# Values of a softmax group in four stretches, a fifth place for exponentials, row DMAs ahead of gathers

## The reference

```python
def _L0_attn_b_ref(x, Wq, Wk, Wv, Wo):
    ...
    q, k, v = (proj(Wq), proj(Wk), proj(Wv))      # 16 heads of 16
    ...                                           # rotary turn of q and k
    att = jnp.einsum('bhqd,bhkd->bhqk', q, k) / math.sqrt(hd)
    mask = jnp.triu(jnp.full((T, T), -jnp.inf, dtype=att.dtype), k=1)
    att = jax.nn.softmax(att + mask, axis=-1)
    out = jnp.einsum('bhqk,bhkd->bhqd', att, v)
    out = out.transpose(0, 2, 1, 3).reshape(B, T, D)
    return out @ Wo.T
x = x + _L0_attn_b_ref(_layernorm(x, axis=-1), L0_attn_b_Wq, L0_attn_b_Wk, L0_attn_b_Wv, L0_attn_b_Wo)
```

## Time and profile before

| | us |
|---|---|
| median of 3 runs (1100.65 to 1104.69) | 1101.19 |
| the profiled execution | 1101.02 |
| its span, first to last instruction | 1099.3 |
| TensorE busy | 1047.7 (95%) |
| ScalarE busy | 617.4 (56%) |
| VectorE busy | 594.2 (54%) |
| GpSimd busy | 489.3 (45%) |

### The profile page before, as it was taken

How to read it: one execution, slowest core, us unless ns; L and a number is a source line. 1 busy time by engine, 2 the same in 40 slices (tenths; PEclk the granted TensorE clock), 3 DMA queues, 4 the chain that set the end, 5 groups by cost and what they waited for, 6 DMA issues and landing times. The chain is left out here.

```text
span 1099.3 us, 33516 instructions
## 1 busy us (share of the span) xinstructions
PE 1047.7 (95%) x14384; PEld 826.2 (75%) x14384; DVE 594.2 (54%) x1326; ACT 617.4 (56%) x1172; POOL 489.3 (45%) x524
## 2 busy tenths in 40 slices
PE   4999999999999999999999999988799999999998
PEld 3888889888888888898888878855444444445787
DVE  5243433334243545545452764598777778785533
ACT  4544444444444555555554666685477677767763
POOL 1454454455454555554553635753133332221346
PEclk9999999999999999999999989999899999999999
DMA  3100100001001012102004120067622333000001
GB/s 134 57 3 3 57 3 30 30 3 49 17 2 50 17 31 72 32 17 86 17 23 141 39 68 1 3 154 199 120 61 60 61 61 61 1 3 1 1 20 58
DMA packets 19613, 50.77 MB, mean 46 GB/s; under 512 B 2687, under 2 KB 13759, under 8 KB 16575
## 3 DMA queue, kind: packets, MB, share of 16 engines
q1 hardware_dynamic: 19470, 48.67, 16.1%
HBM read 37.71 MB, written 10.75 MB: 44 GB/s over the span
## 5 line engine op out<-in xcount | busy, mean ns | idle before, releaser
L1892 DVE TENSOR_REDUCE aa_mx<-aa_S 128x1 f32<-128x640 f32 (+1 forms) x192 | 173.3, 952 | 50.0 <-PE aa_S L1608 48.8
L512 DVE SCALAR_TENSOR_TENSOR la_y<-la_g,la_O 128x512 f32<-128x512 f32 x64 | 41.1, 684 | 238.6 <-PE la_O L692 238.6
L1798 ACT ACTIVATE aa_PT<-keep 128x512 f32<-128x512 f32 (+1 forms) x203 | 110.6, 583 | 46.3 <-PE keep L1632 45.0
L602 PE MATMUL la_R<-a_hTh,WF 128*128 128x512 f32 x384 | 129.0, 401 | 4.3 <-DVE a_hTl L160 4.3
L1532 POOL TENSOR_SCALAR_AFFINE_SELECT aa_PT<-aa_PT 128x256 f32<-128x256 f32 (+1 forms) x112 | 49.3, 440 | 183.2 <-ACT aa_PT L1798 179.8
L298 POOL TENSOR_TENSOR la_qd<-q,la_C 128x512 f32<-128x512 f32 x64 | 81.0, 1288 | 95.0 <-PE la_O L692 95.0
L311 POOL TENSOR_TENSOR la_yl<-la_y,la_yh 128x512 fp32r<-128x512 f32 x62 | 79.2, 1299 | 88.5 <-ACT la_yh L392 88.5
L361 ACT ACTIVATE q<-la_R 128x512 f32<-128x512 f32 x64 | 38.3, 598 | 116.9 <-PE la_R L602 116.9
L519 DVE TENSOR_TENSOR X<-la_R,X 128x512 f32<-128x512 f32 x64 | 44.3, 692 | 92.7 <-PE la_R L602 92.6
L1077 POOL TENSOR_TENSOR f_fl<-f_f,f_fh 128x512 fp32r<-128x512 f32 x48 | 61.8, 1296 | 63.6 <-ACT f_fh L936 63.5
L319 POOL TENSOR_TENSOR fin_sqacc<-fin_sqacc,la_sq 128x512 f32<-128x512 f32 x64 | 86.2, 1347 | 7.9 <-DVE X L1199 3.3
(11 more groups left out here) (288 smaller groups left out, 2776.2 us busy)
## 6 DMA issues: line engine op xcount, KB each, us to landing
la_Wraw<-w_quads_dram SPq DMA_DIRECT2D x7, 1280.0 KB, 5.4
aa_stacks<-k_parts SPq DMA_DIRECT2D x16, 256.0 KB, 6.8
q_parts<-aa_QP SPq DMA_DIRECT2D x8, 384.0 KB, 5.0
aa_stacks<-q_parts SPq DMA_DIRECT2D x8, 384.0 KB, 4.5
k_parts<-aa_KP SPq DMA_DIRECT2D x8, 384.0 KB, 4.3
qw_w<-w_ffn_dram SPq DMA_DIRECT2D x12, 192.0 KB, 2.4
q_ffn<-qw_w SPq DMA_DIRECT2D x12, 192.0 KB, 1.9
X<-hidden_dram SPq DMA_DIRECT2D x4, 512.0 KB, 7.4
```

What stands on the lines that cost most here:

```text
L602: m = pe.matmul(out, a, b, start=n == 0, stop=n == len(pairs) - 1)
L1798: act.activation(PT[:, (NM2 * g + b) % NPT, h:h + nh, 0:w], ST[at % NB][:, 0:nh * w].rearrange("p (h q) -> p h q", h=nh), ACT.Exp, scale=S ...
L1892: dve.reduce_max(out, src, AXX).then_inc(s1_free, 1)
```

## The change

Blocks' values stand in four stretches, of 4, 3, 2 and 3 blocks, behind steps 14, 26 and 34 and behind step 3 of the next group. The places for exponentials become five; room for the fifth comes from V, whose heads are 24 numbers apart and not 32. A matmul still reads 32, of which the last 8 belong to the next head (or to 32 zeros at the end) and give rows of the output that nobody reads. The table `BEHIND` has other numbers. SyncE issues the rows of the second half of g ahead of the gathers of g + 2, and at the start the mask rows of group 1 ahead of the rows of group 0 and the gathers of group 1.

```diff
-        NSL, NPT, NB = 3, 4, 3
+        NSL, NPT, NB, VW = 3, 5, 3, 24
...
-        V = sb("V", [P, NT, SH, 32], F32)
+        Vf = sb("V", [P, NT * SH * VW + 32], F32)
+        V = Vf[:, 0:NT * SH * VW].rearrange("p (t h d) -> p t h d", t=NT, h=SH)
...
-        VALUES_AT = [max(LAST[b | 1] + 3, (LAST + [NST + LAST[0]])[(b | 1) + 1]) for b in range(NM2)]
+        STRETCH = (3, 3, 3, 3, 6, 6, 6, 8, 8, 11, 11, 11)
+        VALUES_AT = [max(LAST[e] + 3, (LAST + [NST + LAST[0]])[e + 1]) for e in STRETCH]
...
-        BEHIND = (0, 1, 2, 4, 5, 6, 9, 10, 11, 13, 15, 17, 19, 21, 22, 23, 24, 26, 28, 30, 31, 33, 35, 37)
+        BEHIND = (0, 2, 3, 4, 6, 8, 10, 12, 13, 14, 15, 17, 19, 21, 23, 25, 26, 27, 29, 31, 33, 34, 35, 37)
...
-            rows(0, 0)
             sp.wait_ge(l_ok, 1)
             ln["turned"](sp)
+            sp.wait_ge(fixed_in, fixed_count(0))
+            fixed(QS[1], 0)
+            fixed(KS[1], 1)
+            rows(0, 0)
             gather_queries(sp, 1, QS[1], q_parts, s_in[1])
             gather_keys(sp, 1, KS[1], k_parts, s_in[1])
-            fixed(QS[1], 0)
-            fixed(KS[1], 1)
...
             for g in range(NG2):
+                rows(g, 1)
                 if g >= 1 and g + 2 < NG2:
                     load(g + 2)
-                rows(g, 1)
...
-            for n in range(4):
-                pool.memset(V[:, 4 * n:4 * (n + 1), :, SD + 1:32], 0.0).then_inc(v0_ok, 1)
+            pool.memset(V[:, :, :, SD + 1:VW], 0.0).then_inc(v0_ok, 1)
+            pool.memset(Vf[:, NT * SH * VW:], 0.0).then_inc(v0_ok, 1)
...
-                    ins = pe.matmul(OB[32 * j:32 * j + 32, q0 - qb * TB:q0 - qb * TB + w], V[:, 8 * (g // NG) + kt, HG * (g % NG) + j, :],
+                    at = ((8 * (g // NG) + kt) * SH + HG * (g % NG) + j) * VW
+                    ins = pe.matmul(OB[32 * j:32 * j + 32, q0 - qb * TB:q0 - qb * TB + w], Vf[:, at:at + 32],
```

More of the change, by code:

```diff
@@ L1775, in projected @@
             def projected(n):
-                act.wait_ge(v0_ok, 5)
+                act.wait_ge(v0_ok, 3)
                 act.wait_ge(vb_ok, n + 1)
```

## The result

| | before | after |
|---|---|---|
| median, us (range, runs) | 1102.94 (1100.65 to 1104.72, 4) | 1123.23 (1119.98 to 1125.18, 4) |
| ratio after / before | | 1.0183, 95% interval 1.0153 to 1.0212 |
| profiled execution, its span | 1101.02, 1099.3 | 1125.15, 1123.4 |
| mean granted clock of that execution | 0.994 | 0.984 |

Slower, by 20.3 us in the medians and 24.1 in the two profiled executions. The other three runs of after took 1121.31, 1119.98 and 1125.18 us at a mean granted clock of 0.992, 0.992 and 0.985.

The account below looks back on a forecast made before the run. TensorE sets the end in attention, with waits for rows and banks. Groups 1 to 5 +11.5, group 6 +3.0, group 7 +1.5, group 0 +1.0, mask rows -1.6, clock -0.7: +14.7 on 1101.02, 1116 us (1105 to 1126).

Parts of the forecast that it names:

- step 4 to 15: First piece of a group's score steps: step 11's wait for row DMAs grows from 0.70 to 1.6 us; +1.05 a group.
- T: Start of score step 4 of a group, right behind the values of the group before; times in a group count from it.
- the two other pieces: Score steps 15 to 27 and 27 to the next 4: forecast 10.0 and 11.5 us a group.
- what brings nothing: V's zero fill, V's step of 24, later gathers of group g + 2: no effect; the fifth place buys no time itself.
- the mask rows: Start of group 1: TensorE's 2.37 us wait for mask rows goes, VectorE then binds; 1.6 us saved.
- the clock: Granted clock at the start, 775 to 782 us: 0.7 us saved, from -0.5 to +2.0.
- falls behind step 11: Rival: the hole at step 11 lowers the clock, 1.5 to 3 us a group lost, 1126 to 1137; chance 0.12.
- groups 6 and 7: Last two attention groups: group 6 +3.0 us, group 7 +1.5 (0 to 3).
- rival of rings that hold: Row wait grows, but score and maximum banks cover the longer stretches: +4.2 us, 1105; chance 0.13.
- 27 to 4: Score step 27 to the next group's step 4: waits for maximum banks, 11.5 us, +0.65 a group.
- 15 to 27: Twelve score steps in a row, then three blocks of values: ScalarE and maximum bank waits, 10.0 us, +0.6 a group.
- faster one: Rival: rows land before TensorE reaches step 11 and both rings hold, saving switches and row waits: 1091; chance 0.06.

Follow-up runs that it names:

- e6: Changed kernel with values of blocks 0 and 1 back behind step 10 (stretches of 2, 2, 3, 2, 3 blocks), new segment table: 1109.41 us, ratio 1.0054.
- e2: Kernel before with one edit: rows of the second half of g issued ahead of the gathers of g + 2: 1100.8 us, ratio 0.9968.
- e14: Kernel before with both SyncE moves (mask rows first, rows ahead of gathers) and nothing else: 1098.23 us, ratio 0.9951.
- e7: Changed kernel with the six pairs of values and old BEHIND table; five places, V of 24 and both SyncE moves stay: 1097.48 us, ratio 0.9949.
- e1: Kernel before with one edit: mask rows of group 1 issued ahead of the rows of group 0 and the gathers of group 1: 1100.33 us, ratio 0.9987.
- e12: Changed kernel with old BEHIND table and eleven stretches, blocks 0 and 1 together and every other block alone: 1103.05 us, ratio 0.9986.
- e4: Changed kernel with the BEHIND table of the kernel before, long stretches kept: 1122.15 us, ratio 1.017.
- e3: Changed kernel with rows of the second half turned and copied at step 3 and not 5: 1119.99 us, ratio 1.0157.
- e13: Changed kernel with rows of the second half turned at step 4, ahead of the copy of the outputs: 1113.63 us, ratio 1.0105.

## Why the prediction was right, and where it was off

**Right: the mechanism of step 4 to 15.** The rows were issued at T + 1.96 and taken at T + 5.76 (forecast 5.6), and the wait is 1.64 (forecast 1.6) in group 3 and 1.53 to 2.06 in groups 1 to 7, without an exception for 6 and 7. The 2.06 of group 4 is over the 1.2 to 1.8 of the text. The segment behind step 14 waited 0.22 (0.3). Step 15 came at 10.41 for 10.1: 0.16 of it are the rows, the rest small pieces between steps 11 and 14. e6 against after prices the move at 1.50, more than the +1.05 of the text, because before the change the wait was 0.70 and in e6 it is none. The Trainium skill, "DMA: Bandwidth & Descriptors", Anatomy of one DMA, with its fixed cost of about 2.0 us on another issuing path, gave an estimate of T + 6.0 from the fourth issue; the measured T + 5.76 is nearer to the 5.6 that came from the rows, and 0.24 from the page.

The two halves of the change worked against each other: with the values in their old place (e2, e14, e7) the rows are there when step 11 is reached, and moving the values away takes the cover under which they land.

**Right: the two other pieces.** 10.03 for 10.0 and 11.52 for 11.5. At step 18 stands 0.29 for 0.45, and the segments behind 26 and 0 wait 0.28 and 0.54 for 0.44 and 0.68. The sums came nearer than their terms: the small waits of the trace are spread over more places than a count step by step gives. The group was 31.96 for 31.6; five of them are 13.1 us over the 146.7 before, where the sum had 11.5, so groups 1 to 5 at full clock are 1.6 over the text. One reading of the text is off without harm: five maxima in 4.55 us are 0.91 each, not 0.86.

**Right: what brings nothing.** Fifth place and V of 24 (e7 against e14). The stretches' price of 0.15 + 1.67 ns a column: four blocks of 1280 columns took 887.05 to 889.34 = 2.29 for 2.28.

**Right with its size unproved: the mask rows.** 2.37 gave way to waits for k and for VectorE. From the first score matmul of group 0 to the projection it takes 10.49 us (767.12 to 777.61) for 12.00 (765.97 to 777.97), 1.5 less for the forecast 1.6. As a time, e1 gives 1.4, and its interval includes no change.

**Off: the clock.** This is the term of the sum that was mis-sized. The text took 0.7 us saved at the start and put falls behind step 11 into a rival (1.5 to 3 us in every group, 0.12). They came in four groups of seven, at 1.22 to 1.43 each: 5.3 of the 9 us that the sum was short. The rival's 1126 and up was not reached in the first measurement and was in the second (1128.11), there through time outside the groups. The forecast's mechanism carried the larger part: 31.96 - 29.32 = 2.64 a group at full clock, 13.1 in groups 1 to 5 and 3.0 in 6 and 7, of 24.1. The rival's chance was too low for a hole that the text itself had sized. At the start, up to step 4 of group 1, the forecast said -1.3 and it was +1.1. Of these 2.4, 1.15 were there at the first score matmul of group 0 already, with a granted clock of 0.83 in 750 to 770 (1.00 before, 0.83 also in e6, e7, e12 and e14). Another 1.1 came between the projection and step 4 of group 1: 34.78 us (777.61 to 812.39) for 33.34, so +1.4, where the text had +0.3 (group 0's +1.0 and the clock's -0.7). The clock gave nothing back there: 0.62 was granted in 778 to 782 for 0.57 before.

That the time stayed inside 1105 to 1126 was in part luck. The falls were left out of the sum, the range had room for them, and the kernel's second measurement, with the same four falls, lies above it.

**Off, the other way:** groups 6 and 7 cost 3.0 and not 4.5. Group 6 is as forecast (977.88 to 1010.96, 33.08 us for 30.19 before: +2.9 for +3.0); it was group 7 that did not cost its 1.5 (33.65 for 33.55). Behind the attention 1.2 more were lost, where nothing was forecast; 0.87 of it is in the first matmuls there, 1.94 us for 1.07, at a clock that had fallen again behind a wait that the kernel before has too, without a fall:

```profile
1044.61 1.94 PE L146 MATMUL f_T<-ident,aa_ATT 128*128 128x128 f32 x8 [1.35 <-PEq L1275]
```

So: 5.3 for the falls, 0.4 for group 4's longer wait, 2.4 at the start, 1.6 for groups 1 to 5, -1.5 for 6 and 7, and 1.2 behind are 9.4, as in the spans (1123.4 - 1099.3 - 14.7).

The rival of rings that hold (1105) is out: 27 to 4 and 15 to 27 grew as counted. The faster one (1091) is out at step 11. But its half that concerns rows is true where their cover stays: in e14 step 11 waits for them in group 4 alone, 0.31 us.

## What to carry to other kernels

Work that seems to interrupt a pipeline may be the cover of a transfer: before merging it elsewhere, read what lands behind it and how long that flies (here 3.80 us from the first of four issues), and price the move by the hole it opens. Fewer switches pay little and longer stretches can cost more: a switch cost 0.12 us net, and merging the later blocks, with the table made for that, cost 1.9 us a group (e7 to e6). A table of places belongs to one layout; it is to be found again when the layout goes back, as 1.35 us a group showed. And a hole of 1.6 us in TensorE costs more than itself when the clock goes down behind it, as it did in four groups of seven. Last, one profile of each side is thin ground for the price of one edit: the wait that e2 seemed to remove was mostly gone in e1 as well.

## What the hardware showed that I had not expected

- A hole of 1.6 to 2.1 us at step 11 was followed, within 1.5 us of its end, by a granted clock of 0.58 to 0.74 over 4 us in four of seven groups (1, 2, 4, 5), in both profiles of after and at the same groups; groups 3, 6 and 7, with 1.53 to 1.64, kept 1.00. With 1.53 to 1.96 in e4 it was two groups of seven, with the 1.02 to 1.13 of e3 also two. The waits of e13, 0.6 us and once 1.02, were followed by none.
- The kernel before is itself not at rest: its medians beside the experiments went from 1101.7 to 1104.5, and single kernels differ by 2 to 10 us between runs (before from 1098.99 to 1108.54), with falls of the clock in 730 to 785 us at changing places.
- Five extra changes between score matmuls and values cost a group only 0.59 us.
- Step 11's wait for the rows was 0.61 to 0.94 us in groups 1 to 5 of the kernel before, and 0, 0, 0.17, about 0.2 and 0.43 in e1, whose rows stand behind the gathers as before.
